# Attention scores as four 64x64 products on TensorE's array, both banks in one piece behind the first transposes

## The chip, the cores and the metric

The kernel runs on one core of one Trainium2 chip. The core has TensorE (matrix products and transposes, results into eight PSUM banks), VectorE (DVE in the profile), ScalarE (ACT), GpSimd (POOL) and SyncE (SP, here for DMAs). Each engine runs its own instructions in order; they wait for one another by semaphores. The metric is the time of one execution on the device, in microseconds, lower is better.

## What is computed

One layer of cross attention and a mixture of experts over 32 sequences of 64 tokens with 128 features, all in float32. Cut to what matters:

```
x = x + attention(layernorm(x), ctx, mask)      # 16 heads of 8 features, keys and values from ctx
x = x + moe(layernorm(x))                       # 16 experts, the best two per token, and a shared expert
attention: q = norm(x) Wq^T, k = ctx Wk^T, v = ctx Wv^T, split in heads
           p = softmax(q k^T / scale, masked keys out);  (p v) Wo^T      # scale = 8 ** -0.5
```

## The kernel before

2048 tokens are 16 tiles of 128 tokens, so a tile holds two sequences (b = 0, 1). Heads are taken in two groups of eight (hg or g = 0, 1). After a prologue that makes queries, keys and values, the attention is a software pipeline: `pipeline` (L290) calls each engine's `step(t, p, on)` for t = 0 to 15, the middle eight in a hardware loop of two turns with four steps each; the step for t = -1 starts the first scores. Within step t an engine works on several tiles: scores and softmax of tile t + 1, transposes and values of tile t, the output projection of tile t - 1, the second norm and the router of tile t - 2 and t - 3. The order inside a step is the order in which the code is written. Then come the experts (L1105 on), some of whose first products lie in the last steps.

Queries and keys are kept with the features of sequence b in rows 64 b to 64 b + 63. For a tile, GpSimd writes `q_blk` (L447): for each head group 128 columns, with the other sequence's rows zero, and `k_blk` (L455): for each head group 8 x 64 columns, each head's keys with the other heads' rows zero. One product per head group (L1039, 128x128 against 512 columns, two passes each since the operands are float32) then fills a bank: rows are both sequences' queries, columns the eight heads' keys.

The engines in one step, in their order:
- TensorE (L1012): scores of bank 0, values as rows L990 (waits for ScalarE's copy `pvt_sb`), four transposes of the first half of the probabilities (L1021, wait for the first exponential), scores of bank 1, attention transposed L995 (waits for VectorE's `att`), four transposes of the second half, L1006, L1000, values (L1030), router L1010.
- VectorE (L789): residual sum L794, router and norm pieces, row maximum of bank 0 (L827), 1/denominator and `att` of tile t - 1 (L836, L838), subtraction of bank 0 (L848), row maximum and subtraction of bank 1.
- ScalarE (L569): block of values, a piece of the experts' weights, copy of the first transposes (L596), `xn` L609 (waits for GpSimd's bias), L613, copy of the second transposes (L596), L619, L620, exponential of bank 0 (L602), `pvt_sb` (L625), exponential of bank 1.
- GpSimd (L482): `q_blk` and, with the norm's small operations between, `k_blk` of tile t + 2, and for each group of four tiles the exponent's scale from the first norm (`rstd1_of`, L425).

## Time and profile before

| | us |
|---|---|
| median of 3 runs | 190.82 (190.80 to 191.46) |
| the profiled execution | 190.56 |
| its span | 188.7 |
| TensorE busy | 173.1 (92%) |
| VectorE busy | 161.4 (85%) |
| ScalarE busy | 130.2 (69%) |
| GpSimd busy | 89.2 (47%) |

The span runs from the first to the last instruction of the profiled execution; what lies around it is 1.9 us. Times of rows count from the span's start. PE is TensorE with its products, PEld its weight loads, which run beside the products. A matmul's record lasts longer than it holds the array, since products are pipelined and their ends are modelled. The granted clock is a share of full speed. A bracket at the end of a row is the idle time of that engine ahead of it and what ended it.

### The profile page before, as it was taken

Reading aid. Unit: us, or ns where it says so; the run is one execution under the profiler, and the core shown is the slowest. Engines: PE = TensorE matmul, PEld = TensorE weight load, DVE = VectorE, ACT = ScalarE, POOL = GpSimd, SP = SyncE. Lnnn points to the kernel's source line nnn. Section 1 sums busy time; section 2 is a strip of 40 time slices with the busy share of each in tenths; the row PEclk is TensorE's granted clock in tenths of the full one; section 3 lists DMA queues with packets and bytes.
Section 4 is the critical chain, followed back from the end, with each engine's and each line's share of the span. In section 5 each row is a group of like instructions: output and inputs, shape, how many; then the busy total and the mean of one; then the engine's idle time right before and its main releaser. Section 6 shows DMA issues by size and latency. Waiting matters only on the chain.

```text
span 188.7 us, 4275 instructions
## 1 busy us (share of the span) xinstructions
PE 173.1 (92%) x1305; PEld 124.9 (66%) x1305; DVE 161.4 (85%) x501; ACT 130.2 (69%) x292; POOL 89.2 (47%) x146
## 2 busy tenths in 40 slices
PE   7887889787999999999999799999999999999963
PEld 7763455455666666666677476788878877788741
DVE  5569999997999999999984899988988899889961
ACT  3195797776899999999889566565556555665631
POOL 7049997369888888888698850400000000000000
PEclk9999999999999999999999999999999999999985
DMA  5999200000000000000003423432534153315201
GB/s 105 288 332 386 96 2 2 3 0 2 3 0 5 0 0 0 0 0 5 0 1 94 147 106 109 118 115 92 152 118 154 70 158 136 130 63 161 62 2 56
DMA packets 12128, 15.43 MB, mean 82 GB/s; under 512 B 1744, under 2 KB 6608, under 8 KB 11984
## 3 DMA queue, kind: packets, MB, share of 16 engines
q1 hardware_dynamic: 10800, 13.79, 22.8%
q10 hardware_dynamic: 1312, 1.46, 2.8%
q8 instruction: 7, 0.11, 0.3%
q14 instruction: 9, 0.07, 0.1%
HBM read 14.06 MB, written 1.18 MB: 81 GB/s over the span
## 4 chain that ended last, share of the span: by engine, by line
PE 55%; DVE 23%; issue 7%; ACT 4%; DMA 4%; POOL 3%; ACTq 1%; DVEq 0%; POOLq 0%
PE bank L1092 31%; PE bank L1039 8%; PE bank L1021 4%; DMA mhalf<-mask_half 4%; PE bank L1030 4%; DVE hid L904 4%; DVE smax L827 4%; DVE prob L848 3%; ACT hid_hi L667 2%; DVE k_all L769 2%; PE bank L1010 2%; PE bank L1000 2%; DVE stats L701 1%; POOL k_blk L455 1%; PE bank L990 1%
## 5 line engine op out<-in xcount | busy, mean ns | idle before, releaser
L1039 PE MATMUL bank<-k_blk,q_blk 128*128 128x512 f32 x64 | 33.9, 614 | 1.3 <-POOL k_blk L455 1.1
L658 ACT ACTIVATE sig<-bank 128x512 f32<-128x512 f32 x36 | 21.5, 599 | 19.1 <-PE bank L1092 18.7
L455 POOL TENSOR_TENSOR k_blk<-k_all,consts_sb 128x512 f32<-128x512 f32 x32 | 33.2, 1058 | 0.0
L667 ACT CAST hid_hi<-hid 128x512 fp32r<-128x512 f32 (+1 forms) x37 | 22.4, 609 | 12.0 <-DVE hid L904 11.9
L1092 PE MATMUL bank<-xt_hi,w_hi 128*128 (+1 forms) x72 | 29.3, 407 | 0.2 <-ACT sig L658 0.2
L896 DVE TENSOR_TENSOR hid_lo<-hid,hid_hi 128x512 fp32r<-128x512 f32 (+1 forms) x37 | 25.1, 680 | 4.3 <-ACT hid_hi L667 4.1
L1092 PE MATMUL bank<-xt_hi,w_lo 128*128 (+1 forms) x72 | 28.2, 392 | 0.0
L1092 PE MATMUL bank<-xt_lo,w_hi 128*128 (+1 forms) x72 | 28.2, 392 | 0.0
L602 ACT ACTIVATE prob<-prob,exp_scale 128x512 f32<-128x512 f32 x32 | 23.8, 744 | 2.9 <-DVE prob L848 2.9
L887 DVE TENSOR_TENSOR hid_u<-sig,bank 128x512 f32<-128x512 f32 x32 | 21.8, 682 | 3.9 <-PE bank L1092 2.5
L904 DVE TENSOR_TENSOR hid<-hid_u,cb 128x512 f32<-128x512 f32 x32 | 23.0, 718 | 0.0
L848 DVE TENSOR_TENSOR prob<-bank,smax 128x512 f32<-128x512 f32 x32 | 22.0, 686 | 0.6
L827 DVE TENSOR_REDUCE smax<-bank 128x8 f32<-128x512 f32 x32 | 21.9, 683 | 0.3 <-PE bank L1039 0.2
L596 ACT COPY prob_t<-bank 128x512 f32<-128x512 f32 x32 | 18.7, 587 | 3.7 <-PE bank L1021 3.0
L1021 PE MATMUL bank<-consts_sb,prob 128*128 128x128 f32 x128 | 19.2, 273 | 0.0
L1092 PE MATMUL bank<-hid_hi,w_hi 128*128 128x512 f32 (+1 forms) x37 | 15.4, 417 | 2.9 <-DVE hid_lo L896 2.9
L1021 PEld LDWEIGHTS bank<-consts_sb,prob 128*128 128x128 f32 x128 | 15.1, 141 | 1.2 <-issue 1.1
L1092 PEld LDWEIGHTS bank<-xt_hi,w_hi 128*128 128x128 f32 x72 | 13.6, 189 | 3.3 <-issue 0.6
L1092 PEld LDWEIGHTS bank<-xt_hi,w_lo 128*128 128x128 f32 x72 | 13.5, 188 | 3.0
L1092 PEld LDWEIGHTS bank<-xt_lo,w_hi 128*128 128x128 f32 x72 | 13.6, 189 | 2.6
L1092 PE MATMUL bank<-hid_lo,w_hi 128*128 128x512 f32 (+1 forms) x37 | 14.7, 396 | 0.0
L1092 PE MATMUL bank<-hid_hi,w_lo 128*128 128x512 f32 (+1 forms) x37 | 14.6, 395 | 0.0
(117 smaller groups left out, 333.2 us busy)
## 6 DMA issues: line engine op xcount, KB each, us to landing
cb<-comb_rows SPq DMA_DIRECT2D x64, 128.0 KB, 2.9
w_moe_sb<-w_moe SPq DMA_DIRECT2D x1, 1296.0 KB, 10.3
ctxt_sb<-ctx_t SPq DMA_DIRECT2D x4, 256.0 KB, 8.7
xt_sb<-x_t ACTq DMA_DIRECT2D x4, 256.0 KB, 8.4
x_sb<-x SPq DMA_DIRECT2D x4, 256.0 KB, 11.0
out<-x_sb SPq DMA_DIRECT2D x3, 256.0 KB, 3.1
w_moe_sb<-w_moe SPq DMA_DIRECT2D x1, 432.0 KB, 7.9
w_att_sb<-w_att SPq DMA_DIRECT2D x1, 264.0 KB, 3.9
```

Of the source, the lines that this page charges most:

```text
L455: last = nc.gpsimd.tensor_tensor(k_blk[p][:, g, :, :], k_all[:, bass.ds(t, 1), g, :].broadcast_to([P, HG, S]), hmask_sb.rearrange("p (h o) ...
L602: nc.scalar.activation(prob[q][:, g * GN:(g + 1) * GN], prob[q][:, g * GN:(g + 1) * GN], ACT.Exp, scale=exp_scale[:, bass.ds(t + 1, 1)]).t ...
L658: nc.scalar.activation(sig[r][:, :], gate_ps[r][:, :], ACT.Silu).then_inc(s_sig, 1)
L667: nc.scalar.copy(hid_hi[k][:, cols], hid[k][:, cols]).then_inc(s_hid_hi, 1)
L827: nc.vector.tensor_reduce(smax[q][:, g * HG:(g + 1) * HG], score_ps[g][:, :].rearrange("p (h s) -> p h s", s=S), AX_X, ALU.max).then_inc(s ...
L848: nc.vector.tensor_tensor(prob[q][:, g * GN:(g + 1) * GN].rearrange("p (h s) -> p h s", s=S), score_ps[g][:, :].rearrange("p (h s) -> p h ...
L887: nc.vector.tensor_tensor(dst[:, :], sig[r][:, :], up_ps[r][:, :], ALU.mult).then_inc(s_hid_u, 1)
L896: nc.vector.tensor_tensor(hid_lo[k][:, cols], hid[k][:, cols], hid_hi[k][:, cols].bitcast(F32), ALU.subtract).then_inc(s_hid_lo, 1)
L904: nc.vector.tensor_tensor(hid[m % 3][:, :], hid_u[r][:, :], cb[k][:, :], ALU.mult).then_inc(s_hid, 1)
L1021: last = nc.tensor.transpose(pt_ps[h][:, j * P:(j + 1) * P], prob[p][:, c:c + P], ident_sb)
L1039: nc.tensor.matmul(score_ps[g][:, :], q_blk[q][:, g, :, :].rearrange("p b s -> p (b s)"), k_blk[q][:, g, :, :].rearrange("p h s -> p (h s) ...
L1092: last = nc.tensor.matmul(out, w, moving, start=start and k == 0, stop=stop and k == 2)
```

## The change

Query blocks are written without zeros: each sequence's queries stay in their own 64 rows. The scores are four products of 64x64 against 512 columns: sequence b uses rows 64 b on, head group hg gives output rows 64 hg on. A bank now belongs to a sequence, and its rows are the queries of head group 0 and then of head group 1. The four products stand in one piece behind the values as rows and the first transposes, and wait for both subtractions; before, the two products stood apart, one at the head of the step and one behind the first transposes. The exponent's scale is needed in the new order of rows, so it is written into two tables, by four operations on 64 rows in place of one on 128. The values' products take their operands from other places, as many as before.

```diff
-        exp_scale = sb("exp_scale", [P, TILES])
+        exp_scale = [sb(f"exp_scale{b}", [P, TILES]) for b in range(BPT)]
         neg_half = sb("neg_half", [P, GT])
         eps_sb = sb("eps_sb", [P, GT])
+        ones_sb = sb("ones_sb", [P, S])
...
-        q_blk = [sb(f"q_blk{p}", [P, 2, BPT, S]) for p in range(2)]
+        q_blk = [sb(f"q_blk{p}", [P, 2, S]) for p in range(2)]
...
-                nc.gpsimd.tensor_tensor(exp_scale[:, tiles], rstd1[p][:, :], any_scale[:, tiles],
-                                        ALU.mult).then_inc(s_escale, 1)
+                for turned in range(2):
+                    for b in range(BPT):
+                        src = slice(b * S, (b + 1) * S)
+                        hg = 1 - b if turned else b
+                        last = nc.gpsimd.tensor_tensor(exp_scale[b][hg * S:(hg + 1) * S, tiles], rstd1[p][src, :],
+                                                       any_scale[src, tiles], ALU.mult)
+                    last.then_inc(s_escale, 1)
+                    pool.wait_ge(s_escale, 2 * g + turned + 1)
...
-                nc.gpsimd.tensor_tensor(
-                    q_blk[p][:, :, :, :],
-                    q_all[:, bass.ds(t, 1), :, :].rearrange("p o g (c s) -> p (o g) c s", c=1).broadcast_to([P, 2, BPT, S]),
-                    half_mask_sb.rearrange("p (o b e) -> p o b e", o=1, e=1).broadcast_to([P, 2, BPT, S]), ALU.mult)
-
-            def k_blocks(t, p):
+                q = q_all[:, bass.ds(t, 1), :, :].rearrange("p o g s -> p (o g) s")
+                nc.gpsimd.tensor_tensor(q_blk[p][:, :, :], q,
+                                        ones_sb[:, :].rearrange("p (o s) -> p o s", o=1).broadcast_to([P, 2, S]),
+                                        ALU.mult)
...
+                    act.wait_ge(s_escale, 2 * (min((t + 1) // GT + 1, GROUPS) if isinstance(t, int) else GROUPS))
                     act.wait_ge(s_sub[g], t + 2)
                     nc.scalar.activation(prob[q][:, g * GN:(g + 1) * GN], prob[q][:, g * GN:(g + 1) * GN], ACT.Exp,
-                                         scale=exp_scale[:, bass.ds(t + 1, 1)]).then_inc(s_exp[g], 1)
+                                         scale=exp_scale[g][:, bass.ds(t + 1, 1)]).then_inc(s_exp[g], 1)
...
-                    for c in range(GT):
-                        j = h * GT + c
+                    for hg in range(2):
+                        for c in range(GT):
+                            last = nc.tensor.matmul(
+                                pvt_ps[c * PW:(c + 1) * PW, hg * P + h * S:hg * P + (h + 1) * S],
+                                v_blk[p][:, h, hg * GT + c, :], prob_t[p][:, h * GT + c, hg * S:(hg + 1) * S],
+                                start=True, stop=True, tile_position=(0, c * PW))
+                    return last
+
+                def scores():
+
+                    if once and t < 0:
+                        pe.wait_ge(s_blk_first, 1)
+                    else:
+                        pe.wait_ge(s_const, 16)
+                        pe.wait_ge(s_blk, t + 1)
                         for b in range(BPT):
-                            last = nc.tensor.matmul(
-                                pvt_ps[c * PW:(c + 1) * PW, h * P + b * S:h * P + (b + 1) * S], v_blk[p][:, b, j, :],
-                                prob_t[p][:, j, b * S:(b + 1) * S], start=True, stop=True, tile_position=(0, c * PW))
-                    return last
-
-                def scores(g):
-
-                    if not (once and t < 0):
-                        pe.wait_ge(s_sub[g], t + 1)
-                    nc.tensor.matmul(score_ps[g][:, :], q_blk[q][:, g, :, :].rearrange("p b s -> p (b s)"),
-                                     k_blk[q][:, g, :, :].rearrange("p h s -> p (h s)"), start=True,
-                                     stop=True).then_inc(s_score[g], 1)
-
-                if on(-1):
-                    pe.wait_ge(s_blk, t + 2)
-                    scores(0)
-                else:
+                            pe.wait_ge(s_sub[b], t + 1)
+                    for b in range(BPT):
+                        rows = slice(b * S, (b + 1) * S)
+                        for hg in range(2):
+                            last = nc.tensor.matmul(score_ps[b][hg * S:(hg + 1) * S, :], q_blk[q][rows, hg, :],
+                                                    k_blk[q][rows, hg, :, :].rearrange("p h s -> p (h s)"), start=True,
+                                                    stop=True, tile_position=(b * S, hg * S))
+                        last.then_inc(s_score[b], 1)
+
+                if not on(-1):
                     pe.wait_ge(s_sub[0], TILES)
                     gate(0, 0)
                     weights_as_rows(0)
@@ -1056,7 +1070,7 @@
                 if on(0):
                     transposes(0)
                 if on(-1):
-                    scores(1)
+                    scores()
```

TensorE's rows at the head of the loop's first step, before (bank5 and bank6 hold scores; a `waits` names semaphores: s_sub is VectorE's subtraction, s_blk the blocks of GpSimd):

```order
L1038 REGISTER_ALU [waits s_blk]
L1039 MATMUL bank5<-k_blk1,q_blk1 128x512 [waits s_sub0]
L988 REGISTER_ALU
L990 MATMUL bank1<-consts_sb,pvt_sb 128x128 [waits s_pvt_sb]
L990 MATMUL bank1<-consts_sb,pvt_sb 128x128
L1021 MATMUL bank7<-consts_sb,prob0 128x128 [waits s_exp0]
L1021 MATMUL bank7<-consts_sb,prob0 128x128 x3
L1039 MATMUL bank6<-k_blk1,q_blk1 128x512 [waits s_sub1]
L995 MATMUL bank2<-consts_sb,att1 128x128 [waits s_att]
L1021 MATMUL bank0<-consts_sb,prob0 128x128 [waits s_exp1]
L1021 MATMUL bank0<-consts_sb,prob0 128x128 x3
```

and now:

```order
L998 MATMUL bank1<-consts_sb,pvt_sb 128x128 [waits s_pvt_sb]
L998 MATMUL bank1<-consts_sb,pvt_sb 128x128
L1025 REGISTER_ALU
L1029 MATMUL bank7<-consts_sb,prob0 128x128 [waits s_exp0]
L1029 MATMUL bank7<-consts_sb,prob0 128x128 x3
L1055 MATMUL bank5<-k_blk1,q_blk1 64x512 [waits s_sub0,s_sub1,s_blk,s_const]
L1055 MATMUL bank5<-k_blk1,q_blk1 64x512
L1055 MATMUL bank6<-k_blk1,q_blk1 64x512 x2
L1003 MATMUL bank2<-consts_sb,att1 128x128 [waits s_att]
L1029 MATMUL bank0<-consts_sb,prob0 128x128 [waits s_exp1]
L1029 MATMUL bank0<-consts_sb,prob0 128x128 x3
```

Both score banks moved behind the four transposes into bank7, L990's transposes (now L998) became the first work of the step, and the transposition of `att` (now L1003) stands behind all four score products.

GpSimd's rows at the end of step 2 and in step 3, before:

```order
L455 TENSOR_TENSOR k_blk0<-k_all,consts_sb 128x512 x2
L429 TENSOR_TENSOR rstd1_1<-veps1_1,neg_half 128x4 [waits s_veps1]
L432 TENSOR_TENSOR exp_scale<-rstd1_1,any_scale 128x4 [waits s_any,s_rstd1]
L510 TENSOR_TENSOR xt2_lo<-xt2_0,xt2_hi 128x128 [waits s_xt2_hi]
L447 TENSOR_TENSOR q_blk1<-q_all,consts_sb 128x256 [waits s_score1,s_k_sb,s_q_sb]
L490 TENSOR_TENSOR veps2_1<-mv2_1,eps_sb 128x1 [waits s_mv2]
L492 TENSOR_TENSOR rstd2_1<-veps2_1,neg_half 128x1 [waits s_veps2]
L496 TENSOR_TENSOR bias2_1<-neg_mean2_1,rstd2_1 128x1 [waits s_nmean2,s_rstd2]
```

and now:

```order
L431 TENSOR_TENSOR rstd1_1<-veps1_1,neg_half 128x4 [waits s_veps1]
L438 TENSOR_TENSOR exp_scale0<-rstd1_1,any_scale 64x4 [waits s_any,s_rstd1]
L438 TENSOR_TENSOR exp_scale1<-rstd1_1,any_scale 64x4
L438 TENSOR_TENSOR exp_scale0<-rstd1_1,any_scale 64x4 [waits s_escale]
L438 TENSOR_TENSOR exp_scale1<-rstd1_1,any_scale 64x4
L518 TENSOR_TENSOR xt2_lo<-xt2_0,xt2_hi 128x128 [waits s_xt2_hi,s_escale]
L456 TENSOR_TENSOR q_blk1<-q_all,ones_sb 128x128 [waits s_score1,s_k_sb,s_q_sb]
L498 TENSOR_TENSOR veps2_1<-mv2_1,eps_sb 128x1 [waits s_mv2]
L500 TENSOR_TENSOR rstd2_1<-veps2_1,neg_half 128x1 [waits s_veps2]
L504 TENSOR_TENSOR bias2_1<-neg_mean2_1,rstd2_1 128x1 [waits s_nmean2,s_rstd2]
L463 TENSOR_TENSOR k_blk1<-k_all,consts_sb 128x512 x2
```

The scale of the exponent became four rows in two pairs, the second pair behind a wait for the first, ahead of everything that GpSimd does in the next step, the bias of the second norm (L496, now L504) among it.

## Rows read from the trace of the kernel before

**Rows 1.** The page: busy time of each engine, and the chain that ended last
```profile
PE 173.1 (92%) x1305; PEld 124.9 (66%) x1305; DVE 161.4 (85%) x501; ACT 130.2 (69%) x292; POOL 89.2 (47%) x146
...
PE 55%; DVE 23%; issue 7%; ACT 4%; DMA 4%; POOL 3%; ACTq 1%; DVEq 0%; POOLq 0%
PE bank L1092 31%; PE bank L1039 8%; PE bank L1021 4%; DMA mhalf<-mask_half 4%; PE bank L1030 4%; DVE hid L904 4%; DVE smax L827 4%; DVE prob L848 3%; ACT hid_hi L667 2%; DVE k_all L769 2%; PE bank L1010 2%; PE bank L1000 2%; DVE stats L701 1%; POOL k_blk L455 1%; PE bank L990 1%
```

**Rows 2.** Busy time of each engine in the stage from 70 to 80 us
```profile
core 0: us, PE busy (x) PEld busy (x) DVE busy (x) ACT busy (x) POOL busy (x), PEclk, DMA share, GB/s
...
70.00:80.00 10.00, 10.00 (x113) 6.75 (x110) 9.40 (x43) 9.43 (x26) 8.74 (x17) 1.00 0.00 0
```

**Rows 3.** The chain in the stretch from 56 to 66 us, in order of time
```profile
by line: PE bank L1039 42.2%; PE bank L1021 20.8%; PE bank L1030 14.5%; PE bank L990 6.6%; PE bank L1010 6.5%; PE bank L1000 6.0%; PE bank L995 3.1%; PE bank L1006 2.2%; issue 2.0%
...
60.65 0.22 PE bank L990 x2
60.87 0.44 PE bank L1021 x4
61.31 0.86 PE bank L1039 x2
```

**Rows 4.** Timeline of one tile: start us, duration us, engine, line, operation, idle before
```profile
74.64 0.69 DVE L827 TENSOR_REDUCE smax<-bank 128x8 f32<-128x512 f32 x1
...
75.53 0.29 DVE L838 TENSOR_TENSOR att<-bank,inv_den 128x128 f32<-128x128 f32 x1
...
75.88 0.14 PEld L995 LDWEIGHTS bank<-consts_sb,att 128*128 128x128 f32 x1 [0.65 <-DVE att L838]
...
76.69 0.59 ACT L596 COPY prob_t<-bank 128x512 f32<-128x512 f32 x1 [0.17 <-PE bank L1021]
...
78.11 0.38 ACT L625 COPY pvt_sb<-bank 128x256 f32<-128x256 f32 x1
78.14 0.17 DVE L797 TENSOR_TENSOR logit<-bank,bias_sb 128x16 f32<-128x16 f32 x1 [0.20 <-PE bank L1010]
...
78.54 0.14 PEld L990 LDWEIGHTS bank<-consts_sb,pvt_sb 128*128 128x128 f32 x1 [0.31 <-ACT pvt_sb L625]
...
79.17 0.69 DVE L827 TENSOR_REDUCE smax<-bank 128x8 f32<-128x512 f32 x1
```

**Rows 5.** By line (min/median/max ns), and timeline of TensorE: full and tiled products
```profile
L1039 PE MATMUL bank<-k_blk,q_blk x64: 592/592/697, 16.7 to 93.8; 128*128 128x512 f32 x64
L959 PEld LDWEIGHTS bank<-xt_sb,wqc_sb x32: 132/136/137, 7.8 to 21.2; 128*64 128x64 f32 x32
L959 PE MATMUL bank<-xt_sb,wqc_sb x32: 379/379/430, 7.9 to 21.4; 128*64 128x256 f32 x32
L983 PE MATMUL bank<-w_att_sb,ctxt_sb x32: 275/275/377, 9.7 to 24.5; 128*128 128x128 f32 x32
...
13.47 1.16 PE L983 MATMUL bank<-w_att_sb,ctxt_sb 128*128 128x128 f32 x8
14.56 1.08 PE L959 MATMUL bank<-xt_sb,wqc_sb 128*64 128x256 f32 x8
...
76.99 0.79 PE L1030 MATMUL bank<-prob_t,v_blk 128*32 128x64 f32 x32
```

**Rows 6.** Timeline of VectorE: first row maximum of tiles 2, 5 and 15
```profile
30.50 0.68 DVE L827 TENSOR_REDUCE smax<-bank 128x8 f32<-128x512 f32 x1
...
47.18 0.69 DVE L827 TENSOR_REDUCE smax<-bank 128x8 f32<-128x512 f32 x1
...
93.56 0.68 DVE L827 TENSOR_REDUCE smax<-bank 128x8 f32<-128x512 f32 x1
```

**Rows 7.** Timeline of GpSimd: the bias of tile 1
```profile
43.69 0.19 POOL L496 TENSOR_TENSOR bias<-neg_mean,rstd 128x1 f32<-128x1 f32 x1
```

**Rows 8.** Timeline of ScalarE: the copy pvt_sb of tiles 0 and 3
```profile
28.93 0.37 ACT L625 COPY pvt_sb<-bank 128x256 f32<-128x256 f32 x1
...
45.88 0.39 ACT L625 COPY pvt_sb<-bank 128x256 f32<-128x256 f32 x1
```

More of the change, by code:

```diff
@@ L65, in sem @@
             return stack.enter_context(nc.semaphore(name))
-        consts_sb = sb("consts_sb", [P, P + HG + 2 + EXPERTS])
+        consts_sb = sb("consts_sb", [P, P + HG + EXPERTS])
         ident_sb = consts_sb[:, 0:P]
         hmask_sb = consts_sb[:, P:P + HG]
-        half_mask_sb = consts_sb[:, P + HG:P + HG + 2]
-        iota_sb = consts_sb[:, P + HG + 2:]
+        iota_sb = consts_sb[:, P + HG:]
         bias_sb = sb("bias_sb", [P, EXPERTS])
@@ L202, in build_program @@
         s_k_sb = sem("s_k_sb")
+        s_blk_first = sem("s_blk_first")
         s_blk = sem("s_blk")
@@ L417, in _ @@
             nc.gpsimd.memset(neg_mean_sb[:, :], -1.0 / D).then_inc(s_half, 1)
+            nc.gpsimd.memset(ones_sb[:, :], 1.0).then_inc(s_half, 1)
             for p in range(2):
@@ L422, in _ @@
                 .then_inc(s_zero[1], 1)
-            pool.wait_ge(s_half, 4)
+            pool.wait_ge(s_half, 5)
             def rstd1_of(g):
@@ L445, in q_block, with k_blocks @@
                     pool.wait_ge(s_score[1], t - 1)
-                nc.gpsimd.tensor_tensor(
-                    q_blk[p][:, :, :, :],
-                    q_all[:, bass.ds(t, 1), :, :].rearrange("p o g (c s) -> p (o g) c s", c=1).broadcast_to([P, 2, BPT, S]),
-                    half_mask_sb.rearrange("p (o b e) -> p o b e", o=1, e=1).broadcast_to([P, 2, BPT, S]), ALU.mult)
-            def k_blocks(t, p):
+                q = q_all[:, bass.ds(t, 1), :, :].rearrange("p o g s -> p (o g) s")
+                nc.gpsimd.tensor_tensor(q_blk[p][:, :, :], q,
+                                        ones_sb[:, :].rearrange("p (o s) -> p o s", o=1).broadcast_to([P, 2, S]),
+                                        ALU.mult)
+            def k_blocks(t, p, written):
                 for g in range(2):
@@ L458, in k_blocks @@
                         hmask_sb.rearrange("p (h o) -> p h o", o=1).broadcast_to([P, HG, S]), ALU.mult)
-                last.then_inc(s_blk, 1)
+                last.then_inc(written, 1)
             mask_ctx(1)
@@ L465, in _ @@
             q_block(0, 0, first=True)
-            k_blocks(0, 0)
+            k_blocks(0, 0, s_blk_first)
             mask_ctx(2)
@@ L470, in _ @@
             q_block(1, 1, first=True)
-            k_blocks(1, 1)
+            k_blocks(1, 1, s_blk)
             LOW_WEIGHTS = ((0, 1, 2), (3, 4), (5, 6), (7, 8))
@@ L497, in step @@
                 if on(-2):
-                    k_blocks(t + 2, p)
+                    k_blocks(t + 2, p, s_blk)
                     if isinstance(t, int) and t < GROUPS - 1:
@@ L599, in exponentials @@
                 def exponentials(g):
-                    act.wait_ge(s_escale, min((t + 1) // GT + 1, GROUPS) if isinstance(t, int) else GROUPS)
+                    act.wait_ge(s_escale, 2 * (min((t + 1) // GT + 1, GROUPS) if isinstance(t, int) else GROUPS))
                     act.wait_ge(s_sub[g], t + 2)
                     nc.scalar.activation(prob[q][:, g * GN:(g + 1) * GN], prob[q][:, g * GN:(g + 1) * GN], ACT.Exp,
-                                         scale=exp_scale[:, bass.ds(t + 1, 1)]).then_inc(s_exp[g], 1)
+                                         scale=exp_scale[g][:, bass.ds(t + 1, 1)]).then_inc(s_exp[g], 1)
                 if on(0):
@@ L1198, in host_layout @@
     head_mask = (head_of_row[:, None] == np.arange(HG)[None, :]).astype(np.float32)
-    half_mask = (np.arange(P)[:, None] // S == np.arange(2)[None, :]).astype(np.float32)
     iota = np.tile(np.arange(EXPERTS, dtype=np.float32), (P, 1))
@@ L1206, in host_layout @@
         "w_att": c(w_att), "router_bias": c(a["L0_ffn_router_bias"].reshape(1, EXPERTS)), "w_moe": c(w_moe),
-        "consts": c(np.concatenate([ident, head_mask, half_mask, iota], axis=1)),
+        "consts": c(np.concatenate([ident, head_mask, iota], axis=1)),
     }
```

## The prediction

> **What bounds the kernel now.** I read the page first. TensorE is busy 92% of the span, VectorE 85%, ScalarE 69%, and the chain of work that ended last lies 55% on TensorE, with the score products (L1039) its second line at 8% [rows 1]. The change works in the attention part, 16 tiles from 16.7 to about 100 us, so I read its stages next. In the stage from 70 to 80 us TensorE counts as busy all the time, VectorE 9.40 and ScalarE 9.43 of 10 us, at full clock [rows 2]: three engines near their limit. The chain cut to 56 to 66 us is TensorE alone, 42.2% of it L1039; its pieces give the array time of each step: 0.22 us for the two transposes L990, 0.44 us for four L1021, 0.86 us for one score product of two passes [rows 3]. Read only so far, the change should help: it would take up to 0.86 of the 1.72 us of scores per tile off the fullest engine.
>
> So I followed one tile in order of time [rows 4]. The period is 79.17 - 74.64 = 4.53 us. VectorE waits 0.20 us in it (at L797), ScalarE 0.17 us (at L596). If TensorE cost nothing, the period could fall only to 4.53 - 0.17 = 4.36 us. The reader is to see something else too: the row maximum L827 starts at 74.64 although the values-as-rows L990 and the transposes L1021 ahead of it are from the same stretch. It needs neither, because the product of its bank is issued at the very start of TensorE's step, ahead of L990, and its wait (the subtraction of the same bank one tile before) was over long ago.
>
> **The change, part by part.**
>
> *The place of the scores* (the term that decides). Both banks' products now stand behind L990, which waits for the copy pvt_sb (ScalarE L625), and behind the first transposes, which wait for the first exponential (L602). The wait for both subtractions is added too, but VectorE is through with them when it turns to L797 at 78.14, before L625 ends at 78.49. Queued behind the scores stands L995, which waits for att (VectorE L838), and VectorE computes att only behind the row maximum of the new scores. Queued behind L995 are the second transposes, and ScalarE's L596, L602 and L625 stand behind these in its order. That closes a ring of one turn per tile. I walk it with durations of [rows 4]:
> - row maximum to the end of att: 74.64 to 75.53 + 0.29 = 75.82, 1.18 us
> - att to the weight load of L995 at 75.88, the transposes, and L596's start at 76.69: 0.87 us
> - L596, two copies and the first exponential, then L625 from 78.11 to its end at 78.49: 1.80 us
> - L625's end to L990's load at 78.54, and 0.06 us until its data runs: 0.11 us. Today L990 then waits for the array, which the first bank's score product still holds; that is gone
> - L990 and four L1021: 0.22 + 0.44 = 0.66 us [rows 3]
> - a change of array shape, 128 columns to 64: 0.14 us, worked out below
> - the first bank's products: 0.86 us, and 0.165 us from the last pass's slot to its end (a record lasts 592 ns, a slot 427) [rows 5], then 0.05 us to VectorE: 1.07 us
>
> Sum 1.18 + 0.87 + 1.80 + 0.11 + 0.66 + 0.14 + 1.07 = 5.83 us. I take 5.8. The ring is longer than today's 4.53 us by 1.3 us, and no other work can shorten it: each part waits for the one before. So TensorE's saved time turns into waiting in front of L990 and L995.
>
> *The four 64x64 products.* The trace shows no product on half of the rows; it shows column tiles. L959 makes four products on two tiles of 64 columns: eight passes of 256 columns in 1.08 us (the row at 14.56). A pass of 256 columns is half of 427 ns, 0.214 us; one by one eight would take 1.71 us, two at a time 4 x 0.214 + 0.165 = 1.02 us. So two run together, though both passes of a product belong to one tile. L1030 on four tiles of 32 columns makes 32 passes of 64 columns (0.053 us each, 1.71 us in all) in 0.79 us [rows 5]. A bank in the new kernel is two column tiles of the same rows, thus like L959: four passes of 512 columns in 2 x 0.427 = 0.86 us. Whether the second bank runs beside the first (whole block 0.86 us) or after it (1.71 us) matters little: its maximum stands on VectorE behind the first maximum and att, at least 1.18 us after the first bank is ready, and L995 waits for att anyway. For the first bank alone the bounds are 0.43 us (if half the rows halved the work) and 1.71 us (nothing together); I take 0.86, the row nearest in shape.
>
> The Trainium skill speaks against this reading: "TensorE: Matmul & The Clock Gate", in Part 3 (Packing small matmuls), says that a weight load overlaps running matmuls only when its row group differs. The two tiles of a bank share their rows, so by that rule a load (137 ns in L959's form) would be exposed in each of two rounds. L959's 1.08 us has no room for it, so the trace disagrees.
>
> *The change of shape.* L983 (128 columns) begins at 13.47 and its last record ends at 14.63, so that record starts at 14.63 - 0.275 = 14.355 and its slot of 0.11 us (half of L990's 0.22) ends at 14.465. L959's first record lasts 0.430 from 14.56, where the full-speed one lasts 0.379, so its data runs from 14.61: 0.145 us lost [rows 5]. The change back, ahead of L995, is hidden in the wait for att.
>
> *The values' order* (L1030): the same 32 passes, four column tiles still in turn: nothing either way, bounds +-0.1 us per tile.
>
> *GpSimd.* The query block writes half the elements: 0.1 to 0.2 us less per tile, hidden, since GpSimd is busy 8.74 of 10 us [rows 2] and its work for a tile is a tile ahead. The exponent's scale takes four operations per group in two waiting pairs in place of one. They are as small as L496 (0.19 us [rows 7]), with a wait between: 0.5 to 0.7 us more. Three such groups lie in the first tiles. Two are covered; the last stands ahead of the bias L496 at 43.69 us, for which ScalarE waits there: on the path once, about 0.6 us.
>
> **The sum.** I count by the start of the first row maximum of a tile [rows 6]. From tile 5 (47.18) to tile 15 (93.56) are ten periods, 46.4 us today; some contain extra VectorE work or a loop's turn, which the ring's waits absorb. Ten turns of 5.8 us take 58.0: +11.6 us. Before: tile 2 is at 30.50 today; by the ring it follows L625's end (28.93 + 0.37 = 29.30 [rows 8]) by 0.11 + 0.66 + 0.14 + 1.07 = 1.98 us, at 31.3: 0.8 late. On the way to tile 3 VectorE has extra work that hides the ring (the ring is shorter in these early steps, too): 0 to 0.3 more, I take 0.15, so 0.95 late. Tile 5: ScalarE waits for the bias at 43.88 and then comes to L625, which ends at 45.88 + 0.39 = 46.27 [rows 8]; 1.98 us behind it is 48.25, in place of 47.18. The bias itself follows VectorE's work of tile 3, 0.95 late, and GpSimd's 0.6 us: 49.8, so tile 5 is 2.6 late. What follows tile 15 (gates in place of scores) is unchanged and only moves. Total 2.6 + 11.6 = +14.2 us. The profiled execution took 190.56 us (188.7 span and 1.9 around it); it becomes 204.8, and the median of 190.82 becomes 205.0 us.
>
> **The rivals.**
> 1. *The ring, but milder* (0.14): the first bank is ready in less than 0.86 us, or the shape change is free. With 0.43 us and no switch the turn is 5.26: 0.57 x 11 = 6 us less, about 199 us. For: no row shows half-height products. Against: a record's time follows the columns that stream.
> 2. *The passes of a bank don't run together as L959's do* (0.10). (a) The weight load of each of the two rounds, 0.137 us in L959's form [rows 5], is exposed: 0.27 us per turn, 3.5 us in 13 turns, 208.5 us (0.03). (b) Only neighbours overlap, 1.28 us for the bank, or nothing does, 1.71 us: 0.42 to 0.85 us per turn, 210.5 to 216 us (0.07). Against both: L959 and L1030. (a) is what the skill's rule above would make of it.
> 3. *TensorE is the bound and the saving shows* (0.04): faster. Its place is the wait ahead of L827. It decides if the first bank is done when VectorE is through with its small operations, at 74.64 in today's tile; then the period falls to ScalarE's 4.36 us, 0.17 x 10 less, 189 us. For: the chain of [rows 3]. Against: L625 ends at 73.97 (one period before 78.49), and 1.98 us of TensorE work behind it end at 75.95, before the ring's growth is even counted.
> 4. *TensorE's clock falls* (0.03) in its new waits of 1 to 1.5 us. The waits of today leave it at 1.00 [rows 2]; at half clock the ring's three pieces on TensorE (0.66, 0.86 and the 0.44 of the second transposes) double: 2 us per tile, about 230 us.
>
> **The numbers.** The ring as walked has 0.67, with 203 to 207.5 us; the rest (0.02) is no change. A measurement of this kernel tells about 0.5%, 1 us, from none. Slower: 0.67 + 0.14 + 0.10 + 0.03 = 0.94; faster 0.04; same 0.02. The range 199 to 210.5 leaves out most of rivals 2 to 4.
>
> **What would show it.** Right: a period of 5.8 us between first row maxima in the loop; VectorE waiting about 1.2 us ahead of L827 (now of another line number) for the score products; TensorE waiting ahead of L990's successor for pvt_sb by some 0.65 us and ahead of L995's for att by 0.7 to 1.5; nearly the same time behind the attention part. Wrong step by step: the first bank's products far from 0.86 us; a gap ahead of them that isn't 0.14; tile 5 later by other than 2 to 3 us. The whole forecast is wrong if VectorE's wait for the scores stays under 0.3 us.

## The result and the profile after

The changed kernel takes 207.51 us (median of 4 runs, 206.62 to 208.80) against 191.14 us (4 runs on the same chip, 190.80 to 191.63): ratio 1.0883, 95% interval 1.0826 to 1.0941. It is slower, as forecast; the time lies in the forecast range (199 to 210.5) and 2.5 us above the value. The profiled execution took 206.62 us, its span 204.7, 16.0 us more than before.

The page of the changed kernel (parts 1, 2 and 5; the last column of part 5 is the idle time ahead of a group). Line numbers are some 8 to 16 higher: L835 is the row maximum, L846 att, L998 the values as rows, L1003 att transposed, L1029 the transposes of the probabilities, L1055 the scores, L604 the copy prob_t, L633 the copy pvt_sb.

```profile
PE 166.8 (82%) x1369; PEld 118.4 (58%) x1369; DVE 161.0 (79%) x501; ACT 129.4 (63%) x292; POOL 89.3 (44%) x159
...
PEclk9999999995599999999999999999999999999997
...
L835 DVE TENSOR_REDUCE smax<-bank 128x8 f32<-128x512 f32 x32 | 22.0, 686 | 15.9 <-PE bank L1055 15.9
...
L1003 PE MATMUL bank<-consts_sb,att 128*128 128x128 f32 x16 | 5.3, 334 | 17.8 <-DVE att L846 17.8
```

TensorE is busy 6.3 us less than in [rows 1], so the cheaper products are real. Yet VectorE now waits 15.9 us in all ahead of the first row maxima for the scores, and TensorE 17.8 us ahead of the att transpose for VectorE: two engines waiting for each other in turn is how a ring looks in a page. The stage of [rows 2], 70 to 80 us, at full clock:

```profile
70.00:80.00 10.00, 6.95 (x104) 5.03 (x104) 8.29 (x40) 6.94 (x19) 6.06 (x13) 1.00 0.00 0
```

TensorE has gone from 10.00 to 6.95 us busy and ScalarE from 9.43 to 6.94; the fullest engine is VectorE with 8.29, so none is at its limit. One tile in order of time, to hold against [rows 4]:

```profile
78.91 0.38 ACT L633 COPY pvt_sb<-bank 128x256 f32<-128x256 f32 x1
...
79.34 0.44 PE L998 MATMUL bank<-consts_sb,pvt_sb 128*128 128x128 f32 x2 [0.46 <-ACT pvt_sb L633]
...
79.62 0.60 PE L1029 MATMUL bank<-consts_sb,prob 128*128 128x128 f32 x4
...
80.15 1.09 PE L1055 MATMUL bank<-k_blk,q_blk 64*64 64x512 f32 x8
...
81.27 0.69 DVE L835 TENSOR_REDUCE smax<-bank 128x8 f32<-128x512 f32 x1 [1.27 <-PE bank L1055]
...
82.16 0.29 DVE L846 TENSOR_TENSOR att<-bank,inv_den 128x128 f32<-128x128 f32 x1
...
82.51 0.33 PE L1003 MATMUL bank<-consts_sb,att 128*128 128x128 f32 x1 [1.27 <-DVE att L846]
...
83.31 0.58 ACT L604 COPY prob_t<-bank 128x512 f32<-128x512 f32 x1 [0.17 <-PE bank L1029]
...
84.73 0.38 ACT L633 COPY pvt_sb<-bank 128x256 f32<-128x256 f32 x1
```

The reader is to walk it: pvt_sb ends at 79.29, the row maximum starts 1.98 us later at 81.27, att ends at 82.45 (1.18), L604 starts at 83.31 (0.86), pvt_sb ends at 85.11 (1.80). The turn is 5.82 us; the forecast had 1.98, 1.18, 0.87 and 1.80. All eight passes of the four 64x64 products last 1.09 us together, from the first record's start to the last one's end.

The first row maxima of tiles 4, 5 and 6, to hold against [rows 6] (that of tile 15 starts at 110.4), then the stage around tile 5 (busy time of each engine as in [rows 2], with the granted clock third from the end):

```profile
41.99 0.69 DVE L835 TENSOR_REDUCE smax<-bank 128x8 f32<-128x512 f32 x1 [0.20 <-PE bank L1055]
...
51.34 0.69 DVE L835 TENSOR_REDUCE smax<-bank 128x8 f32<-128x512 f32 x1 [2.32 <-PE bank L1055]
...
57.97 0.69 DVE L835 TENSOR_REDUCE smax<-bank 128x8 f32<-128x512 f32 x1 [0.96 <-PE bank L1055]
```

```profile
39.00:44.00 5.00, 3.27 (x37) 1.79 (x30) 4.70 (x29) 2.71 (x7) 3.00 (x10) 1.00 0.00 0
44.00:49.00 5.00, 3.61 (x43) 3.14 (x43) 2.40 (x16) 3.69 (x10) 3.86 (x8) 0.62 0.00 0
49.00:54.00 5.00, 3.73 (x17) 1.74 (x16) 2.61 (x7) 1.31 (x5) 2.63 (x4) 0.50 0.01 3
```

From 45.2 to 55.4 us the granted clock is 0.50, its lower level (1.2 GHz). Tile 4 to 5 takes 9.35 us there and tile 5 to 6 6.63; every later turn takes 5.82 or 5.83. Ahead of the fall TensorE waited twice, for att and then for xn, which ScalarE could compute only behind GpSimd's bias; in the low stretch the score block takes 1.99 us:

```profile
43.23 0.33 PE L1003 MATMUL bank<-consts_sb,att 128*128 128x128 f32 x1 [1.27 <-DVE att L846]
...
44.62 0.19 POOL L504 TENSOR_TENSOR bias<-neg_mean,rstd 128x1 f32<-128x1 f32 x1
...
45.39 0.47 PE L1014 MATMUL bank<-consts_sb,xn 128*128 128x128 f32 x1 [1.40 <-ACT xn L617]
...
47.42 0.37 ACT L633 COPY pvt_sb<-bank 128x256 f32<-128x256 f32 x1 [0.46 <-PE bank L1037]
...
49.32 1.99 PE L1055 MATMUL bank<-k_blk,q_blk 64*64 64x512 f32 x8
```

### The profile page after: what moved, and what is told of

It is laid out like the page before. It is cut to its first block, busy times and chain, and to the rows that moved or that the text cites. A ratio compares the mean times of both kernels' runs of the same rounds, so it can differ in the third digit from the quotient of the medians.

```text
span 204.7 us, 4442 instructions
## 1 busy us (share of the span) xinstructions
PE 166.8 (82%) x1369; PEld 118.4 (58%) x1369; DVE 161.0 (79%) x501; ACT 129.4 (63%) x292; POOL 89.3 (44%) x159
## 3 DMA queue, kind: packets, MB, share of 16 engines
HBM read 14.06 MB, written 1.18 MB: 74 GB/s over the span
## 4 chain that ended last, share of the span: by engine, by line
PE 50%; DVE 17%; ACT 13%; issue 10%; DMA 4%; POOL 3%; ACTq 2%; DVEq 0%; POOLq 0%
PE bank L1106 28%; PE bank L1055 6%; PE bank L1029 6%; DVE smax L835 4%; DMA mhalf<-mask_half 4%; DVE hid L912 3%; PE bank L998 3%; ACT pvt_sb L633 2%; ACT hid_hi L675 2%; PE bank L1003 2%; DVE att L846 2%; ACT prob L610 2%; PE bank L1037 2%; ACT v_all L572 1%; DVE prob L856 1%
## 5 line engine op out<-in xcount | busy, mean ns | idle before, releaser
L835 DVE TENSOR_REDUCE smax<-bank 128x8 f32<-128x512 f32 x32 | 22.0, 686 | 15.9 <-PE bank L1055 15.9
L463 POOL TENSOR_TENSOR k_blk<-k_all,consts_sb 128x512 f32<-128x512 f32 x32 | 34.0, 1084 | 0.0
L1106 PE MATMUL bank<-xt_hi,w_hi 128*128 (+1 forms) x72 | 29.3, 407 | 0.1
L604 ACT COPY prob_t<-bank 128x512 f32<-128x512 f32 x32 | 18.8, 592 | 3.3 <-PE bank L1029 3.1
L1003 PEld LDWEIGHTS bank<-consts_sb,att 128*128 128x128 f32 x16 | 2.3, 141 | 31.4 <-DVE att L846 31.3
L1029 PE MATMUL bank<-consts_sb,prob 128*128 128x128 f32 x128 | 20.2, 282 | 0.0
L1003 PE MATMUL bank<-consts_sb,att 128*128 128x128 f32 x16 | 5.3, 334 | 17.8 <-DVE att L846 17.8
L1055 PE MATMUL bank<-k_blk,q_blk 64*64 64x512 f32 x128 | 18.3, 644 | 0.4 <-POOL k_blk L463 0.4
L1029 PEld LDWEIGHTS bank<-consts_sb,prob 128*128 128x128 f32 x128 | 15.8, 147 | 0.9 <-issue 0.8
L518 POOL TENSOR_TENSOR xt_lo<-xt,xt_hi 128x128 fp32r<-128x128 f32 (+1 forms) x16 | 8.0, 499 | 18.3 <-ACT xt_hi L628 18.1
L621 ACT COPY att_t<-bank 128x128 f32<-128x128 f32 x16 | 4.2, 263 | 17.9 <-PE bank L1003 17.8
```

The source lines that it names most:

```text
L463: last = nc.gpsimd.tensor_tensor(k_blk[p][:, g, :, :], k_all[:, bass.ds(t, 1), g, :].broadcast_to([P, HG, S]), hmask_sb.rearrange("p (h o) ...
L835: nc.vector.tensor_reduce(smax[q][:, g * HG:(g + 1) * HG], score_ps[g][:, :].rearrange("p (h s) -> p h s", s=S), AX_X, ALU.max).then_inc(s ...
L1029: last = nc.tensor.transpose(pt_ps[h][:, j * P:(j + 1) * P], prob[p][:, c:c + P], ident_sb)
L1055: last = nc.tensor.matmul(score_ps[b][hg * S:(hg + 1) * S, :], q_blk[q][rows, hg, :], k_blk[q][rows, hg, :, :].rearrange("p h s -> p (h s) ...
L1106: last = nc.tensor.matmul(out, w, moving, start=start and k == 0, stop=stop and k == 2)
```

## The experiments

Each ratio is against the kernel before, run on the same chip (190.05 to 190.35 us), with its 95% interval. A turn is the time between first row maxima of two tiles in the steady part; "before" has 4.52 us.

### The place alone, the shape alone

**Place alone.** The kernel before with both full products behind the first transposes.

```diff
-                if on(-1):
-                    pe.wait_ge(s_blk, t + 2)
-                    scores(0)
-                else:
+                if not on(-1):
...
                 if on(-1):
+                    pe.wait_ge(s_blk, t + 2)
+                    scores(0)
                     scores(1)
```

> The kernel before with the place alone: both full-size score products (blocks with zeros, banks by head group) stand behind the first transposes, waiting for both subtractions. Ring theory: the same ring without the change of shape, 5.83 - 0.14 = 5.69 us per turn, and without the extra scale operations: 202 to 204 us, more if the clock falls as in the changed kernel. Rival (the tiled form is what costs): no tiles here, so within 2 us of the kernel before, up to 193 us.

201.56 us, 0.4 under what I expected, ratio 1.0587 (1.0539 to 1.0634). The turn is 5.67 us, with the clock at 1.00 up to 194 us. The chain of one turn (start us, us, what; "issue" is time in which an engine waited for nothing the profile shows):

```profile
75.08 0.44 PE bank L990 x2
75.52 0.44 PE bank L1021 x4
75.96 0.87 PE bank L1039 x2
...
76.86 0.05 DVE smax L827
...
77.74 0.30 DVE att L838
...
78.09 0.33 PE bank L995
78.42 0.45 PE bank L1021 x4
...
80.33 0.37 ACT pvt_sb L625
...
80.75 0.44 PE bank L990 x2
```

The chain goes through TensorE, VectorE, TensorE, ScalarE and back to L990: the ring of the forecast, without the new shape. The place costs 11.4 us by itself.

**Shape alone.** The changed kernel with bank 0's products at the head of the step (behind a product of one column that carries the wait) and bank 1's behind the first transposes.

```diff
-                def scores():
+                def scores(b):
...
+                        if b == 0:
+                            pe.wait_ge(s_blk, t + 1)
+                            pe.wait_ge(s_sub[0], t + 1)
+                            nc.tensor.matmul(score_ps[0][:, 0:1], ident_sb, half_sb[:, 0:1], start=True, stop=True)
+                        pe.wait_ge(s_const, 16)
+                        pe.wait_ge(s_sub[b], t + 1)
...
-                if not on(-1):
+                if on(-1):
+                    scores(0)
+                else:
...
-                    scores()
+                    scores(1)
```

> The changed kernel with the 64x64 products back in the old places: those of the first bank at the head of TensorE's step (behind one product of one column that carries the wait), those of the second bank behind the first transposes. The new shape and the new query blocks, scales and value products stay, the new place and the one piece go. Theory (the place made the kernel slow, the shape only adds its changes of shape, now twice per tile): a turn per tile of 4.8 to 5.0 us, 195 to 198 us. Rival (a bank's 64x64 products cost much more than the full product when they run alone, since only two of the four tiles are busy at once): first scores of a bank to their row maxima over 1.3 us apart, a turn over 5.2 us, over 200 us.

Four runs took 200.48 to 205.91 us, which is too wide for a ratio, and all of them lie over the 195 to 198 us of the theory. In the profiled one the clock is 0.50 from 45.1 to 65.6 us, and tiles 4 to 7 take 8.57, 9.13 and 7.95 us; the steady turn is 5.16 us, between the theory's 4.8 to 5.0 and the rival's 5.2. So I ran it again with the edit of the section on the clock below, by which GpSimd computes the scales a step later:

> The 64x64 products in the old places, a bank at a time, with the scales of exp one step later, so that the low clock that spoilt the comparison of the shape alone has no long wait ahead of it. Theory (alone a bank's products take 1.00 us against 0.86 for a full product, and each block's successor 0.15 us more, so TensorE has no idle time left and bounds the turn): granted clock 1.00, a turn per tile of 5.16 us against 4.52, 196 to 197 us. Rival (the shape costs nothing once the clock stays up): a turn of 4.6 us or less, 190 us.

196.07 us, ratio 1.0292 (1.0237 to 1.0347), a turn of 5.15 or 5.16 us at full clock. The chain of a turn is TensorE alone:

```profile
67.81 1.00 PE bank L1058 x4
68.82 0.37 PE bank L998 x2
69.19 0.44 PE bank L1029 x4
69.62 1.01 PE bank L1058 x4
70.63 0.26 PE bank L1003
...
72.76 0.21 PE bank L1051 x2
```

Two more rows of the chain of [rows 3], from the kernel before, are needed beside it (its turn, too, is TensorE alone):

```profile
59.70 0.95 PE bank L1039 x2
...
62.17 0.16 PE bank L995
```

The bank behind the transposes takes 1.01 us where the full product took 0.86 [rows 3], and L998 behind the other one 0.37 where it took 0.22: 0.15 us into the new shape and 0.15 out of it. The bank at the head takes 1.00 where the full product took 0.95, and L1003, which was L995, 0.26 where it took 0.16. Together that is 0.45 us per tile. The other 0.21 us are L1051, the experiment's own product of one column, which the kernel before does not have; 4.52 + 0.45 + 0.21 = 5.18 us, the measured turn is 5.16. One bank alone (four passes, 1.00 with the change of shape) costs as much as both banks in one piece (eight passes, 0.16 + 0.86 in the timeline above). So the shape saves nothing unless the banks are issued together, and apart it costs 0.45 us per tile of an engine that is already the limit. Without L1051 the turn would be about 4.95 us, an estimate from these rows, within the 4.8 to 5.0 of the first expectation.

### The ring

**Values as rows behind the scores.** If the ring is right, what is taken out of it shortens the turn by its length. The edit moves the call of `values_as_rows(t - 1)` from the head of the step to behind `scores()`.

> The changed kernel with the values as rows moved from ahead of the first transposes to behind the scores, so that the scores wait for the first exponential only and not for pvt_sb. Ring theory: the ring loses 0.27 us (pvt_sb behind the exponential) and the 0.22 us of two transposes: 5.82 - 0.49 = 5.33 us per turn, some 13 turns, about 201 us (199.5 to 202.5). Rival (the turn is set by the wait for both subtractions or by the block's own length): no change, 207.5 us.

201.40 us, ratio 1.0600 (1.0520 to 1.0679); turn 5.34 us. VectorE's wait for the scores falls from 1.27 us to 0.78 or 0.79. This kernel has a low stretch of its own (43.6 to 50.4 us, tile 4 to 5 in 9.09 us), so its time alone would not show the ring; the turn does.

```profile
71.37 0.69 DVE L835 TENSOR_REDUCE smax<-bank 128x8 f32<-128x512 f32 x1 [0.79 <-PE bank L1055]
```

**The block at the head of the step.** The score block stands where bank 0's product was, behind the one-column product.

```diff
-                if not on(-1):
+                if on(-1):
+                    scores()
+                else:
...
-                if on(-1):
-                    scores()
-                else:
+                if not on(-1):
```

> The changed kernel with one thing moved: the four 64x64 score products stand at the head of TensorE's step again, ahead of the values as rows (plus one product of a single column there that carries the waits, under 0.1 us). Ring theory (the place of the scores costs the time): the row maximum no longer hangs behind pvt_sb and the first transposes; the turn falls from 5.82 us to 4.5 to 4.6 us, VectorE waits under 0.3 us for the scores, and the kernel takes 189.5 to 193 us. Rival (the tiled form costs it: shape changes, passes on half the rows): the form is unchanged, so it stays above 200 us.

194.10 us, 1.1 over the range that I expected, ratio 1.0199 (1.0153 to 1.0245); turn 4.70 us, 0.1 to 0.2 over what I expected. The clock was 0.50 from 44.6 to 51.4 us and tile 4 to 5 took 8.57 us. A smaller ring is left, through TensorE's whole second half of the step:

```profile
78.76 0.69 DVE smax L835
...
79.64 0.30 DVE att L846
...
79.99 0.33 PE bank L1003
...
81.24 0.63 PE bank L1037 x32
...
82.19 0.21 PE bank L1051 x2
82.40 1.03 PE bank L1056 x6
```

The 0.21 us of L1051 are the experiment's own one-column product. It lies in this ring, so without it the turn would be about 4.5 us, as in the kernel before; that is an estimate, no run leaves it out.

**att ahead of the row maximum.** The ring needs att to stand behind the new scores' row maximum on VectorE. This run cuts it there and leaves the block where the change put it (with GpSimd's scales a step later, as below).

```diff
-                if on(-1):
-                    row_max(0)
                 if on(1):
                     pv = ...
...
                     for g in range(2):
-                        if g == 1:
-                            row_max(1)
+                        row_max(g)
```

> The changed kernel with the scales of exp one step later, and on VectorE the reciprocal and att of the tile before moved ahead of the first row maximum; the score block stays where the change put it. Theory (the ring closes only because att stands behind the row maximum of the new scores): att is ready while the block still runs, TensorE's wait of 1.27 us ahead of the att transpose goes, and the ring becomes, from the end of pvt_sb, 0.11 + 0.66 + 0.16 + 0.86 + 0.33 + 0.44 us on TensorE and 1.9 on ScalarE, 4.5 us. A turn per tile of 4.5 to 4.6 in place of 5.82 us, VectorE's wait for the scores under 0.5 us, 188 to 191 us against 203.2 for the same kernel with the old order on VectorE and 190.1 for the kernel before. Rival (the transposes and the block in one row are themselves too long, whatever VectorE's order): a turn over 5.2 us, over 196 us.

191.82 us (12 runs), ratio 1.0071 (1.0033 to 1.0109), against 1.0707 (1.0653 to 1.0760) for the same kernel in VectorE's old order. The steady turn is 4.5 to 4.6 us.

```profile
77.29 0.29 DVE L844 TENSOR_TENSOR att<-bank,inv_den 128x128 f32<-128x128 f32 x1
...
77.64 0.33 PE L1000 MATMUL bank<-consts_sb,att 128*128 128x128 f32 x1
77.65 0.69 DVE L835 TENSOR_REDUCE smax<-bank 128x8 f32<-128x512 f32 x1
```

att ends at 77.58, while the block is just ending, and neither L1000 nor L835 has a bracket: both waits are gone. Two calls in another order on VectorE bring back 11 us. It is the strongest evidence that the loss was one of order. What is left over the kernel before is 0.7%, 1.3 us, and over the kernel before with the scales late, below, some 2 us. The profiled execution has one stretch of low clock (50.6 to 54.0 us, tile 5 to 6 in 7.27 us), but that is not all of it: the three of the twelve runs whose mean granted clock was 1.00 took 190.66, 190.70 and 191.44 us, and two of the kernel before at 1.00 on the same chip 189.25 and 189.84. Where the rest comes from was not tested.

### The low clock

**Filling the wait.** Four products of 128 columns without use behind the score block, into the bank of the second transposes.

```diff
                     scores()
+                    if on(0):
+                        for _ in range(4):
+                            nc.tensor.matmul(pt_ps[1][:, 0:P], half_sb[:, :], half_sb[:, :], start=True, stop=True)
```

> The changed kernel with four products of 128 columns on constants behind each step's scores, into the bank that the second transposes overwrite: 0.88 us of TensorE work inside its wait of 1.27 us for att. Clock theory: TensorE's waits are why its granted clock falls to half once near 46 to 56 us; with the fill it stays at 1.00, tiles 5 and 6 lose their extra 2.3 us and the time is about 205 us. Rival (the fall has nothing to do with the waits, or the fill delays att's transposition): unchanged at 207.5 us or longer.

205.64 us, ratio 1.0806 (1.0753 to 1.0858); turn 5.82 us as in the changed kernel. The clock did not stay at 1.00 as expected, but the low stretch shrinks from 10.2 us to 3.4 (47.9 to 51.3 us), and 1.6 us come back (the row maximum of tile 15 starts at 108.83 in place of 110.40 us); tile 4 to 5 still takes 8.39 us. TensorE's wait for xn (1.41 us) is not touched by the fill.

**The scales a step later.** At step 2 GpSimd waits for the variances of group 3 and computes their powers and scales ahead of the bias that ScalarE and then TensorE wait for. The scales are not needed until later tiles, so groups 1 to 3 move by one step.

```diff
-                    if isinstance(t, int) and t < GROUPS - 1:
-                        rstd1_of(t + 1)
+                    if isinstance(t, int) and 1 <= t < GROUPS:
+                        rstd1_of(t)
```

> The changed kernel with the scales of exp one step later, nothing else. Theory (the part of the loss that the forecast lacks, 2.5 us, is the wait for the bias near tile 5 and the low clock that follows it): granted clock 1.00 between 45 and 55 us, tile 4 to 5 about 6.2 in place of 9.34 us, tile 5 to 6 5.85 in place of 6.64, the steady turn unchanged at 5.83; 203.3 to 204.3 us. Rival (the low clock comes from the ring's waits of 1.3 us themselves): the dip stays, 206 us or more.

203.17 us, ratio 1.0707 (1.0653 to 1.0760), turn 5.82. Tiles 4 to 5 and 5 to 6 now take 5.82 us each, and the clock is full from 39 us to the last microsecond. But another appeared, 3.4 us long, ahead of it, and tile 2 to 3 took 6.99 us in place of 5.53:

```profile
34.00:39.00 5.00, 3.46 (x15) 1.56 (x16) 3.36 (x13) 2.50 (x6) 2.72 (x5) 0.66 0.00 0
```

The size of the effect on the time was as expected; "the clock stays at 1.00" holds for 45 to 55 us only.

**One scale product.** ScalarE reads the one table for both banks.

```diff
-                for turned in range(2):
-                    for b in range(BPT):
...
+                nc.gpsimd.tensor_tensor(exp_scale[0][:, tiles], rstd1[p][:, :], any_scale[:, tiles],
+                                        ALU.mult).then_inc(s_escale, 2)
```

> The changed kernel with one product for the scales of exp, over all 128 rows, as the kernel before has it; the scales of the rows whose head group and sequence are swapped are left out (those rows take the scale of another sequence), so its output is not the reference's. Theory (the three further products of 0.20 us make the bias near tile 5 0.8 us later, TensorE's wait for xn 1.40 us long, and the clock falls after it): the clock stays at 1.00 between 45 and 55 us, tile 4 to 5 about 6.4 us, tile 5 to 6 5.85, 203.5 to 204.5 us. Rival (the length of the wait for xn does not decide the clock, or the wait stays over 1.2 us behind the ring): the clock falls again, 206 us or more.

206.25 us, ratio 1.0837 (1.0781 to 1.0894): the total speaks for the rival, the place does not. Tile 4 to 5 takes 6.33 us with the clock at 1.00, as the theory had it, and TensorE waits 0.55 us for xn in place of 1.40. But the clock fell at 29.3 us and stayed low to 39.5:

```profile
29.00:34.00 5.00, 3.73 (x19) 1.72 (x18) 3.00 (x12) 1.75 (x5) 1.98 (x4) 0.53 0.00 2
```

Ahead of that lie other waits of TensorE, 1.12 us for prob_t at 27.39 and 0.58 us for pvt_sb at 28.80. By themselves they do not explain it: the changed kernel has the same two waits, at 27.33 and 28.74, and its clock stayed at 1.00 there. So with fewer scale products the clock fell all the same, 16 us earlier, and what moved it is not shown.

**Head of the step, scales later.** Both edits together.

> The 64x64 block at the head of the step (the first experiment on the place, 194.1 us), with the scales of exp one step later as well. Theory (TensorE's long wait for the bias near 44 us is followed by the granted clock of 0.50, and both make tile 4 to 5 last 8.58 us): the clock stays at 1.00 between 44 and 51 us, tile 4 to 5 in 5.0 to 5.5 us, 190.5 to 191.5 us in all. Rival (the clock falls there for another reason): tile 4 to 5 stays over 8 us, 193.5 or more.

191.84 us, ratio 1.0126 (1.0081 to 1.0171), 0.3 us above what I expected. The clock stays at 1.00 up to 187 us, tile 4 to 5 takes 4.71 us in place of 8.57, the steady turn is 4.70. Tile 5 to 6 takes 5.94 us in place of 5.32: ScalarE now waits 1.19 us for the bias of the next step.

### A faster version

The same GpSimd edit in the kernel before, where ScalarE waits 2.25 us for the bias.

> The kernel before with GpSimd's scales of exp (powers and products) for groups 1 to 3 computed one step later. Theory (at step 2 GpSimd waits 1.51 us for the variances of group 3, and ScalarE 2.25 us for the bias behind that): the wait of 2.25 us goes, tile 4 to tile 5 in about 4.6 in place of 5.7 us, 1 us less in all: 189.1 us against 190.15. Rival (ScalarE's wait is hidden, something else sets tile 5): no change, 190.1.

189.29 us (10 runs), ratio 0.9977 (0.9948 to 1.0006): not told from no change. So it was run again in five rounds.

> The kernel before with the scales of exp for groups 1 to 3 one step later, the same kernel as in the earlier experiment with that edit, in five rounds. Theory (0.8 to 1.6 us are saved near tile 5, and nothing is added elsewhere): ratio 0.992 to 0.997, with 1 outside its interval. Rival (the saving is lost again at the end of the attention part): ratio within 0.002 of 1.

189.37 us (12 runs), ratio 0.9955 (0.9927 to 0.9983). It is faster in this set, and the two sets together put the gain at 0.2 to 0.5%. Tile 4 to 5 takes 4.79 and 4.52 us in the two profiles in place of 5.68, and tile 5 to 6 5.02 and 5.32 in place of 4.55: half or more of what the first turn gains is lost in the next, where ScalarE now waits 0.9 us for the bias behind the scales. ScalarE's wait for the bias, first in the kernel before, then with the edit (first set):

```profile
43.92 0.49 ACT L609 ACTIVATE xn<-x_sb,bias,rstd 128x128 f32<-128x128 f32 x1 [2.25 <-POOL bias L496]
```

```profile
42.03 0.49 ACT L609 ACTIVATE xn<-x_sb,bias,rstd 128x128 f32<-128x128 f32 x1 [1.03 <-POOL bias L496]
```

## Why the prediction was right, point by point

**The ring** held in each of its terms: forecast 5.83 us a turn, measured 5.82 or 5.83, with VectorE's wait at 1.27 us (about 1.2 forecast), the wait for pvt_sb at 0.46 (0.65), for att at 1.27 (0.7 to 1.5). That it is a ring, and not the sum of two slowed engines, is shown from three sides: the place alone closes it (5.67), taking the values as rows out of it shortens it (5.34), and reordering VectorE opens it (4.6).

**The products** were 0.86 us for the first bank, and the block's two banks run side by side: one bank alone costs the same. The Trainium skill, "TensorE: Matmul & The Clock Gate", Part 3, would have a weight load exposed where two tiles share their row group; the block has 1.09 us from start to end, 0.07 until its data runs and 2 x 0.427 + 0.165 = 1.02 for two rounds, so no load of 0.13 us is exposed. The trace disagrees with that rule. It agrees with the other condition that the same Part gives, by which a load into the background weight buffer is pulled ahead as well; no run here tells whether that is the reason.

**The change of shape** was 0.14 forecast. In the timeline above the transposes hold the array to 79.62 + 0.60 - 0.165 = 80.06, the block's data runs from 80.15 + 1.09 - 1.02 = 80.22: 0.16 us. From 5.67 with full products to 5.82 with the new ones is 0.15. The Trainium skill, "TensorEngine Tiling (Array Packing)", Key Properties, says that a change of tiling mode drains the engine, without a figure; the traces agree in that time is lost at a change, 0.14 to 0.16 us into the new shape and 0.10 to 0.15 us back; they don't show the drain itself.

**Tile 5** is the term that was mis-sized, twice and in opposite directions. Forecast 2.6 us late, measured 51.34 - 47.18 = 4.2. The forecast had tile 2 late by 0.8 us and tile 3 by 0.95; measured are 30.64 - 30.50 = 0.14 and 36.17 - 35.99 = 0.18. It had taken the end of tile 0's pvt_sb from the kernel before (29.30 us), and in the changed kernel that copy ends at 28.22 + 0.37 = 28.59. So the bias came 44.62 - 43.69 = 0.93 us late, not 1.55. GpSimd's rows ahead of it, before and then after:

```profile
40.56 1.02 POOL L429 TENSOR_TENSOR rstd<-veps,neg_half 128x4 f32<-128x4 f32 x1 [1.51 <-DVE veps L709]
41.66 0.20 POOL L432 TENSOR_TENSOR exp_scale<-rstd,any_scale 128x4 f32<-128x4 f32 x1
```

```profile
40.75 1.02 POOL L431 TENSOR_TENSOR rstd<-veps,neg_half 128x4 f32<-128x4 f32 x1 [1.57 <-DVE veps L717]
41.85 0.98 POOL L438 TENSOR_TENSOR exp_scale<-rstd,any_scale 64x4 f32<-64x4 f32 x4
```

VectorE's lateness is passed on in full, and it is only 0.19 us; the scale products and the shorter query block add 0.74 where the forecast had 0.6. Full clock would thus have given 0.93 + 1.07 = 2.0. The run with one scale product, at full clock in this stretch, bears that out: there the row maximum of tile 5 follows TensorE's transposition of xn by 51.91 - 48.13 = 3.78 us, and 45.39 + 3.78 = 49.17 is 2.0 later than 47.18. The other 2.2 us are the low clock, and it took 0.8 us more from tile 5 to 6. The forecast had a falling clock as rival 4, with 0.03, and only as a loss in every tile (230 us). It came in one stretch of the attention part and cost some 3 us. That the time came out only 2.5 us above the value is in part luck: the lateness of tile 3, forecast 0.8 us too long, hides part of it.

**The sum.** Tile 5 +4.2 in place of 2.6; tiles 5 to 15 are 59.1 us against 46.4, +12.7 in place of 11.6 (0.8 of it the low clock); behind tile 15 0.8 us come back, against nothing forecast. 4.2 + 12.7 - 0.8 = 16.1 us, the span's 16.0. The 0.8 us are probably no gain of the change: the kernel before ran at the low clock from 183.1 us to its end at 188.7, and in the first profile with its scales late, which has full clock to the end, the part behind tile 15 takes 94.4 us, as in the changed kernel (94.3), not 95.1. Without the low clock the forecast's method gives 191.1 + 13.0, about 204 us.

**The rivals.** The milder ring and the passes that don't run together are out by the turn and by the block's 1.09 us. That TensorE's saving shows is out: VectorE's wait is 1.27 us, not under 0.3. Place and shape are both losses by themselves, 11.4 us and 6.0 us, of which up to 3 us are the experiment's one-column product (an estimate, 0.21 us in some 14 turns). Together they cost 13.1 us (with the scales late), less than their sum: in one piece behind the ring the shape adds only the 0.15 us from 5.67 to 5.82 to a turn, where apart it adds 0.45.

**What stays open** is why the clock falls. In the profiles it fell once in the attention part in most versions with long waits of TensorE there, at places between 29 and 51 us, and in most, the kernel before among them, again in the last microseconds. It did not fall in the nine steady turns of 5.82 us from tile 6 on, though each has waits of 1.27 and 0.46 us. Two waits near each other, 1.27 and 1.40 us (after) or 1.27 and 1.73 us (the block at the head), stood ahead of the fall; 0.81 and 0.98 us (before) did not bring it. But 1.12 and 0.58 us stood ahead of it in one version and brought nothing in another, and of two waits of 1.75 and 1.76 us one had a fall behind it (att ahead of the row maximum) and one had not (head of the step, scales later). The mean granted clock also differs between runs of one and the same kernel, 0.966 to 1.00 in the twelve runs with att ahead of the row maximum. So TensorE's waits alone do not settle when it falls, and one profile per version can't tell a cause from chance.

## What to carry to other kernels

Before moving work behind a wait, write down for each engine what stands in order behind the moved instruction and follow it round: if the path comes back to its own start, the length of that path is the new time per tile, whatever the engines save. When a ring has closed, look for the cheapest edge to cut; here it was two calls in VectorE's order, not TensorE's. And small array tiles pay only when all of them are issued together: two halves apart cost as much each as the whole, and a change of shape on both sides comes with each.

## What the runs showed of the hardware

- Four 64x64 array tiles ran at once: eight passes of 512 columns in 1.09 us, while two tiles (four passes) alone took as long.
- A change between 128-column and 64-column shape cost 0.14 to 0.16 us into the new shape and 0.10 to 0.15 us back.
- In the attention part the granted clock fell to 0.50 for stretches of 3.4 to 20.5 us, which cost some 1 to 10 us (estimates from the turns inside them). The waits of TensorE ahead of a fall don't decide it alone: the same two waits, 1.12 and 0.58 us, had a fall right behind them in one version and none in another.
